# Nine whole expert tiles of the first four batches are run while the last batches are still being routed and ranked

## The reference

```python
x = x + tanh(g_xattn[0]) * xattn(layernorm(x), ctx_2048, mask)       # softmax(x ctx^T / sqrt(512)) ctx
x = x + tanh(g_ffn[0]) * ffn(layernorm(x))

def ffn(x):                                     # T = 2048 tokens
    probs = softmax(xt @ w_router.T)            # 8 experts
    top_v, top_i = top_k(probs, 2)
    top_v = top_v / sum(top_v)
    comb = zeros(T, 8).at[token, top_i].add(top_v)
    g = einsum('th,eih->tei', xt, w_gate)
    u = einsum('th,eih->tei', xt, w_up)
    return einsum('tei,ehi,te->th', silu(g) * u, w_down, comb)
```

## Time and profile before

| | |
|---|---|
| median of 3 runs | 293.11 us (292.9 to 294.67) |
| the profiled execution's own time | 292.34 us |
| its span | 290.5 us |
| mean granted TensorE clock | 0.944 of full |
| TensorE busy | 254.5 us (88%) |
| VectorE busy | 172.3 us (59%) |
| ScalarE busy | 147.4 us (51%) |
| GpSimd busy | 163.8 us (56%) |
| moved by DMA | 52.08 MB, 179 GB/s on average |

### The profile page before, as it was taken

One profiled execution on the slowest core, in us unless ns is written; L12 is line 12 of the kernel. 1 busy time (PEld: TensorE's weight loads), 2 busy tenths in 40 slices (PEclk: granted clock), 3 DMA queues, 4 the chain that ended last, 5 costly groups with the idle time before them and its releaser, 6 DMA issues.

```text
span 290.5 us, 5453 instructions
## 1 busy us (share of the span) xinstructions
PE 254.5 (88%) x1501; PEld 216.1 (74%) x1501; DVE 172.3 (59%) x650; ACT 147.4 (51%) x310; POOL 163.8 (56%) x151
## 2 busy tenths in 40 slices
PE   0999998999999975366999999999999999999940
PEld 1777875687777645356899999899999999999920
DVE  4477779999987899970444444444444554444420
ACT  3469865787765645300455554454444455444430
POOL 1256557556564448316066686874857747748460
PEclk9999999999999978557999999999999999999985
DMA  6996999789988229006157576885985858958582
GB/s 219 381 386 192 325 353 282 295 265 336 301 302 296 82 104 287 4 1 184 38 81 145 103 136 123 143 143 94 171 178 93 168 114 143 154 98 163 109 142 36
DMA packets 25950, 52.08 MB, mean 179 GB/s; under 512 B 5248, under 2 KB 5376, under 8 KB 25920
## 3 DMA queue, kind: packets, MB, share of 16 engines
q0 software_dynamic: 8304, 19.83, 37.0%
q1 hardware_dynamic: 13008, 23.50, 24.7%
q10 hardware_dynamic: 4608, 8.39, 7.6%
HBM read 33.81 MB, written 17.89 MB: 178 GB/s over the span
## 4 chain that ended last, share of the span: by engine, by line
PE 63%; DVE 23%; issue 5%; ACT 3%; DMA 2%; POOL 1%; ACTq 0%; POOLq 0%; DVEq 0%
PE S L1073 9%; PE S L1074 9%; PE S L1077 9%; PE A L1063 5%; PE PO L946 4%; DVE st L609 4%; PE S L935 4%; DVE X L655 3%; DVE TB L721 3%; DVE TA L714 2%; PE PL L1096 2%; DVE dd L675 2%; PE PO L1098 1%; PE PO L1096 1%; PE PL L1100 1%
## 5 line engine op out<-in xcount | busy, mean ns | idle before, releaser
L435 POOL DMA_INDIRECT out<-YT,IXI x36 | 56.8, 1577 | 42.1 <-issue 20.1
L1073 PE MATMUL S<-WGh,XTh 128*128 x144 | 52.3, 363 | 0.9 <-issue 0.8
L1074 PE MATMUL S<-WGl,XTh 128*128 x144 | 49.3, 342 | 0.0
L409 POOL DMA_INDIRECT XG<-x2s,IXG x39 | 38.5, 986 | 18.0 <-issue 9.4
L875 DVE TENSOR_TENSOR H<-SG,S 128x192 f32<-128x192 f32 x36 | 12.7, 354 | 48.5 <-ACT SG L548 40.9
L379 POOL TENSOR_TENSOR WGl<-WGl,WGh 128x512 fp32r<-128x512 f32 x24 | 30.6, 1280 | 14.9 <-ACT WGh L504 14.8
L548 ACT ACTIVATE SG<-S 128x192 f32<-128x192 f32 x36 | 11.9, 330 | 50.3 <-PE S L1077 47.6
L370 POOL TENSOR_TENSOR rs<-mv,CS 128x1 f32<-128x1 f32 x32 | 17.6, 551 | 31.2 <-DVE mv L615 31.2
L946 PE MATMUL PO<-CX,PT 128*128 128x512 f32 x64 | 32.8, 637 | 2.0 <-ACT PT L477 2.0
L868 DVE TENSOR_TENSOR XTl<-A,XTh 128x512 fp32r<-128x512 f32 x37 | 25.6, 691 | 13.0 <-ACT XTh L541 7.9
L1077 PE MATMUL S<-WGh,XTl 128*128 x144 | 31.3, 340 | 0.0
(11 more groups left out here) (153 smaller groups left out, 535.8 us busy)
## 6 DMA issues: line engine op xcount, KB each, us to landing
WGl<-in_wgu SPq DMA_DIRECT2D x24, 256.0 KB, 6.2
X<-in_x SPq DMA_DIRECT2D x16, 256.0 KB, 5.3
CT<-in_ctxt SPq DMA_DIRECT2D x8, 512.0 KB, 6.7
CX<-in_ctxn SPq DMA_DIRECT2D x8, 512.0 KB, 5.4
out<-X ACTq DMA_DIRECT2D x16, 256.0 KB, 5.7
x2s<-Y ACTq DMA_DIRECT2D x16, 256.0 KB, 5.2
WD1l<-in_wd SPq DMA_DIRECT2D x8, 256.0 KB, 5.6
WS<-in_wd SPq DMA_DIRECT2D x8, 256.0 KB, 4.6
```

Of the source, the lines that this page charges most:

```text
L409: pool.indirect_dma_start(out=XG[:, j % NX, :], out_offset=None, in_=x2s, in_offset=bass.IndirectOffsetOnAxis(ap=IXG[:, j:j + 1], axis=0))\
L435: pool.indirect_dma_start(out=out, out_offset=bass.IndirectOffsetOnAxis(ap=IXI[:, j:j + 1], axis=0), in_=YT[:, j % NB, :], in_offset=None, ...
L1073: pe.matmul(o, XTh[:, j % 2, c, :], WGh[:, bass.ds(e, 1), c, :], start=(c == 0), stop=False)
L1074: pe.matmul(o, XTh[:, j % 2, c, :], WGl[:, bass.ds(e, 1), c, :], start=False, stop=False)
```

## The change

The list is made in two parts. After batch 3, `whole()` counts only full tiles of 128 slots in the first four batches; at least 9 exist (`NE = 4 * EB - 7`), and the first 9 go into `IXE` and `ERE`, while the other batches are still in the pipeline. The attention loops stop after step 16; what was left of the tail (attention of tiles 14 and 15, the routing of the last tiles, the ranking of batches 4 to 7, the second list `IXG`, `IXI`, `ERL` with up to 30 tiles) is put by hand into the first tiles of the expert stage, on VectorE by the table `SIDES` (steps before `xlo`, before `hlo` and after it, for each tile). All 40 weight units are now handled in the attention stage, three a step. The scatter index of the early tiles is the same as their gather index.

PSUM is used more tightly, since both kinds of work run together: `tx` has one bank, `th` writes into the bank of `gu`, `down` has one bank. Result buffers are seven, two of them in `WS`. The first gathers wait for the stores that read the `X` slot under their buffer. In GpSimd's queue the gather of tile j+8 follows the add of tile j (before: j+6). An add now always waits for the add two tiles back; it waits for its neighbour only where the expert changes and the first tokens and last tokens of the two tiles allow a common token. Of `exp` for the mixing weights, batches 6 and 7 go to GpSimd as powers of e (`odds`). The two groups of warm-up matmuls ahead of the expert stage (15 and 32) are gone.

```diff
-NB = 5
+NB = 7
-SPLIT = [0, 1, 1] + [2] * 15 + [1] * 4
-NUA = NU - 4
-HOLD = [3, 5, 7, 9]
+SPLIT = [0, 1, 2] + [3] * 12 + [1]
+EB = 4
+NE = 4 * EB - 7
+NL = 32
+SIDES = [(2, 2, 5), (2, 2, 3), (1, 1, 2), (1, 1, 2), (2, 2, 2), (2, 2, 3), (1, 3, 4), (2, 1, 4)] + [(0, 0, 0)] * 31
...
+            def stored(*tiles):
+                pool.wait_ge(s_y2, max(tiles) + 1)
+                for k in tiles:
+                    pool.wait_ge(s_so[k % NXT], 16 * (k // NXT + 1))
+            def fence(j):
+                bits, i = (early, j - 1) if j < NE else (turns[(j - NE - 1) // 15], (j - NE - 1) % 15)
+                with pool.If((bits & (1 << i)) != 0):
+                    landed(j - 1)
...
+                if s == NTK:
+                    pool.wait_ge(s_ixe, 1)
+                    pool.wait_ge(s_sy[0], 16 * EB)
+                    pool.wait_ge(s_sy[1], 16 * EB)
+                    pool.wait_ge(s_scb[0], 16 * EB)
+                    stored(9, 10)
+                    gather(0)
...
                     pool.wait_ge(s_y, j + 1)
-                    if j:
-                        fence(j)
+                    if j >= 2:
+                        landed(j - 2)
+                    if j == NE:
+                        landed(j - 1)
+                    elif j:
+                        fence(j)
...
+                    if j + NX + 2 == NE:
+                        pool.wait_ge(s_ixg, 1)
+                        pool.wait_ge(s_sy[0], 16 * 8)
+                        pool.wait_ge(s_sy[1], 16 * 8)
+                        pool.wait_ge(s_scb[1], 16 * (B - EB))
+                    if j + NX + 2 < NT:
+                        gather(j + NX + 2)
...
+            tp(14)
+            first_list()
+            score(15)
+            pv(14)
+            rt(12)
+            t2(13)
+            tp(15)
...
+            tx(0)
+            pv(15)
+            rt(13)
+            own, live = experts(0, ERE, 0), None
+            pe.wait_ge(s_wl, NU)
             for j in range(NT):
                 with lives(pe, live, j):
                     gu(j, own[j])
+                    if j == 0:
+                        t2(14)
+                    if j == 1:
+                        t2(15)
+                        rt(14)
                     if j + 1 < NT:
                         tx(j + 1)
+                    if j == 0:
+                        cum(5)
+                    if j == 2:
+                        tab(5)
+                        cum(6)
+                    if j == 4:
+                        cum(7)
+                        count()
+                    if j == 5:
+                        tab(6)
+                    if j == 6:
+                        last_list()
+                        tab(7)
...
                     if j >= 1:
                         down(j - 1, own[j - 1])
+                    if j == 1:
+                        rt(15)
+                    if j == 6:
+                        last_rows()
                     th(j)
+                    if j == 0:
+                        tab(4)
```

More of the change, by code:

```diff
@@ L266, in units @@
         def units(s):
-            return range(*[min(NUA, sum(SPLIT[:max(0, n)])) for n in (s, s + 1)])
+            return range(*[min(NU, sum(SPLIT[:max(0, n)])) for n in (s, s + 1)])
         def rows(to, k):
@@ L411, in gather, with landed @@
                     .then_inc(s_g[j % NX], 16)
[L413 to L424 removed]
+            def landed(j):
+                pool.wait_ge(s_add[j % NB], 16 * (j // NB + 1))
@@ L425, in _ @@
+            stored(11)
+            gather(1)
+            rstd(mv2, 14, rs2, s_st2, s_rs2)
+            stored(12)
+            gather(2)
+            rstd(mv2, 15, rs2, s_st2, s_rs2)
+            odds(6)
+            stored(13)
+            gather(3)
+            pool.wait_ge(s_tne, 1)
+            early = pool.value_load(TNE[0:1, 0:1], min_val=0, max_val=(1 << 13) - 1)
+            stored(14, 15)
+            for j in range(4, NX):
                 gather(j)
-            pool.wait_ge(s_tn, 1)
@@ L887, in coef @@
                     dve.wait_ge(s_y, j - 3)
-                link(dve.tensor_tensor(cj8[:, j % 2, :], XG[:, j % NX, D:DW], EJ[:, j, :], ALU.mult))
+                link(dve.tensor_tensor(cj8[:, j % 2, :], XG[:, xg(j), D:DW], EJ[:, j, :], ALU.mult))
                 dve.reduce_sum(cj[:, j % 4:j % 4 + 1], cj8[:, j % 2, :], AX.X).then_inc(s_cj, 1)
-            xlo(0)
+            for s in range(NTK + 1):
+                main = []
+                if s == NTK:
+                    main.append(first_rows())
+                if 0 <= s - 3 < NTK:
+                    main.append(x2(s - 3))
+                if s == NTK:
+                    main.append(first_experts())
+                if s + 2 < NTK:
+                    main.append(st1(s + 2))
+                if 0 <= s - 3 < NTK:
+                    main.append(nbias(mv2, rs2, nb2, s - 3, s_rs2, s_nb2))
+                if s == 2 * EB + 7:
+                    main.append(table())
+                if 0 <= s - 1 < NTK:
+                    main.append(rowmax(s - 1))
+                if s + 2 < NTK:
+                    main.append(nbias(mv1, rs1, nb1, s + 2, s_rs1, s_nb1))
+                if 0 <= s - 1 < NTK:
+                    main.append(norm(s - 1))
+                if s == 2 * EB + 4:
+                    side.append(slots(EB - 2))
+                if s >= 6 and s % 2 == 0:
+                    side.append(top2((s - 6) // 2))
+                if s == 2 * EB + 5:
+                    side.append(braid(slots(EB - 1), whole()))
+                if s >= 8 and s % 2 == 0 and s not in (2 * EB + 4, 2 * EB + 6):
+                    side.append(slots((s - 8) // 2))
+                if s >= 6 and s % 2 == 0:
+                    side.append(ranks((s - 6) // 2))
+                if s >= 7 and s % 2 == 1:
+                    side.append(coefs((s - 7) // 2))
+                weave(queue(*main), s >= 2 * EB + 4)
@@ new lines, in steps, with first_xlo @@
+            def steps(n):
+                for _ in range(n):
+                    while side and next(side[0], side) is side:
+                        side.pop(0)
+            def first_xlo():
+                xlo(0)
+                yield
+            side += [coefs(5), top2(6), taken()]
+            weave(queue(x2(14), first_xlo(), nbias(mv2, rs2, nb2, 14, s_rs2, s_nb2), x2(15)), 2)
+            side += [slots(5), ranks(6), coefs(6),
+                     braid(slots(6), queue(top2(7), braid(ranks(7), coefs(7)))),
+                     braid(slots(7), left()), last_tiles()]
@@ L1025, in _ @@
-                if 0 <= s - 3 < NTK:
-                    t2(s - 3)
-                if s >= 7 and s % 2 == 1 and (s - 7) // 2 < B and s != NTK + 3:
-                    cum((s - 7) // 2)
-                if s == 2 * B + 5:
-                    pe.wait_ge(s_ms, B)
-                    pe.wait_ge(s_lc, B - 1)
-                    for t in range(2 * RB, 2 * B):
-                        pe.matmul(PL[:, 0:8], onesb, MS[:, t // 2, t % 2, :], start=(t == 2 * RB), stop=False)
-                    pe.matmul(PL[:, 0:8], onesb, Rn[:, RB, :], start=False, stop=True).then_inc(s_cnt, 1)
```

645 lines of the change are left out of this document (387 added, 258 removed).

## The result

| | before | after |
|---|---|---|
| median | 293.0 us (4 runs) | 300.82 us (298.31 to 302.35, 4 runs) |
| ratio | | 1.0254, 95% interval 1.0214 to 1.0294 |
| profiled execution, its span | 292.34, 290.5 us | 300.13, 298.3 us |

280.3 us was forecast. The span can be cut at five places that can be read off TensorE's queue. `tp(14)` and the transposes of gathered tiles (`tx`) are marks that both kernels have; "forecast" is the prediction's sum, moved from the first expert matmul to the transpose ahead of it (1.4 us before it).

What follows compares the result with a forecast made beforehand. TensorE was taken to bound both stages, with a VectorE ranking chain making the gap between them. Pieces 96.2 + 5 + 11.5 + 46.4 + 109.5 + 9.9 gave a 278.5 us span, 280.3 us forecast; range 271 to 289.5.

Steps and rivals of the forecast that it cites:

- Piece 1: Attention stage up to tp(14): 96.2 us plus 5 for the third weight unit, bounds 0 and 14.
- (a): GpSimd's queue has room, but 13 more subtractions hold up VectorE by 0.33 us each, 4.3 us.
- (c): Attention-stage DMA: 2.10 MB a step becomes a second bound of equal height; late loads cost a little now and then.
- Each subtraction blocks in full: Rival, attention stage: each of 13 subtractions stops VectorE for its length, 14 instead of 5 us, 289.3; chance 0.16.
- The rival in series: Attention stage: third unit's rounding and subtraction both unhidden in the step's chain, 23.5 instead of 5 us, 298.8; chance 0.06.
- piece 4: Other 27 expert tiles: 109.5 us; the adds' new rule moves nothing, their 3.29 us wait being hidden GpSimd idle time.
- Piece 2 and 3: From tp(14) to the first expert matmul, 11.5 us; then nine early tiles with the moved side work, 46.4 us.
- Piece 5: Tail after the last matmul (last yev, last add and its landing): 9.9 us, unchanged.
- Faster: Whole kernel faster by over 1%: forecast, nothing gives way, late start and over half of full blocking; chance 0.87.
- The signs that I named beforehand: Wrong if attention steps exceed 6.7 us, TensorE awaits last list or gather 9, clock falls to 0.50, yev awaits adds.

Runs made afterwards that it cites:

- e7: Changed kernel with the subtraction of every third weight unit (12 units) cut to 8 of 512 columns, loads and roundings kept: 286.89 us, ratio 0.9767.
- e1: Kernel before with only three weight units a step added (36 by step 13), no early tiles: 298.58 us, ratio 1.0196.
- e2: Changed kernel with the third subtraction of a step moved behind the step's second power in GpSimd's queue: 296.55 us, ratio 1.0141.
- e11: e9 and e8 together, on the changed kernel, both leaving out what they do: 278.94 us, ratio 0.9512.
- e9: e7 with the top-two search of batch 3 put ahead of batch 2's slots in VectorE's ranking work in step 12: 284.13 us, ratio 0.9719.
- e8: Changed kernel with its first nine adds sent to spare rows, without their neighbour waits (results left out): 297.22 us.
- e3: Changed kernel with GpSimd's wait for the second list moved from behind add 1 to behind add 5, two gathers an add after it: 305.99 us, ratio 1.047.
- e10: Changed kernel, whole computation, with the third subtraction behind the second power and batch 3's top-two search first in step 12: 294.10 us, ratio 1.0016.

## Why the prediction was wrong

*What bounds the kernel.* Right: the gap was a chain on VectorE, and it went: `tp(14)` to `tx(0)` fell from 37.1 to 8.4 us.

*Piece 1, up to `tp(14)`: the step that failed.* "I take 5: the 4.3 of (a), and a little for (c)"; it was 21.8, over the upper bound of 14. Three things were wrong in it.
- The price. I took the mean holding up of VectorE for each subtraction (9.0 / 27 = 0.33) and added it up. e7 measured 1.0 us for each of twelve, e1 1.6 for each of nine in the old kernel, with their loads and roundings; why e1's is higher is not shown. By the estimate above an added subtraction held VectorE up for 0.9 us (11.5 / 13; in e1 (18.5 - 9.4) / 9 = 1.0), three times the mean. That mean came from two subtractions a step, one ahead of each power. The third made two in a row ahead of the second power, so that two instructions were held in turn and the power of the next tile came behind them, as the step above shows. e2 prices this place at 4.3 of A's 13.9 us. That the other subtractions of a step had been mostly hidden, and this one could not be, fits these sums, but no run tests it.
- The bound. "Each subtraction blocks in full" (14 us) counted the instruction that is held, not what stands in order behind it (the bias, ScalarE's `Y`, the power of the other tile), nor TensorE's clock behind an idle stretch. The rival in series, 298.8 us at a chance of 0.06, came within 2 us of the result, but its total met it by luck: the moved ranking and piece 4 made part of the loss, and it had nothing on them. Its place was right, GpSimd's subtraction on the step's path. How much that cost by itself lies between e7's 12 to 14 us and the 21 of e1's rate (13 x 1.6), beside its 23.5; none of it is the rounding, which e7 kept while its steps 6 to 11 were 0.2 us longer than before.
- The moved ranking. Up to `tp(14)` I gave it no price at all, since I took the diff's double rate for filling. One search moved was worth 5.5 us of `tp(14)` in the profiled executions (105.60 to 100.06; e11, with the same attention stage as e9, has 101.89, which makes it 3.7) and 2.8 in the medians. With A and this gone `tp(14)` is still 3.9 to 5.7 us later than before, of which step 13 makes 2.8. That this is near my 5 is luck: I had put 4.3 of them on the very subtractions that these runs leave out.

DMA, my (c), took no part that can be seen, as e7 shows. The estimated 5.9 us that the prediction drew from 358 GB/s was no floor for a step: over 14 us of e7 this core moved 376 GB/s, at which the step's 2.10 MB take 5.6 us.

*Piece 2 and 3.* Right: 57.9 us forecast for both, 55.1 measured up to the first matmul of tile 9. The side work fits under the nine tiles; the tightened PSUM shows in no wait (TensorE's longest from `tx(0)` to `tx(9)` is 1.43 us, for tile 0's product `H`). The second list came in time for TensorE: gather 9 started 34.6 us after the first expert matmul, where I had the list at about 33. GpSimd stood still 11.64 us for it, which I had put down as harmless.

*Piece 4.* "The adds' new rule moves nothing on this path" was wrong by 5.9 us. I took the wait of 3.29 us for rare and hidden, which it is behind add 9, in the long runs of one expert. Among the first nine it is not rare: seven adds stood behind the list, and four of them and add 9 waited, so that GpSimd, which came out of its stop with little lead, lost the rest. I had priced gather 9 and not gathers 12 to 17. e8 and e3 show it from both sides.

*Piece 5.* Right, 9.9 and 10.1.

*The chances.* Faster had 0.87, all of it on piece 1, for which I had one indirect row. The signs that I named beforehand did show: steps longer than 6.7 us, and waits for gathers (of tiles 12 to 17, not of tile 9). The clock's lower level showed too, behind idle stretches of the attention stage, which was not the place that I had named. Longer `MS` and `comb` did not show.

## What to carry to other kernels

When work is added to an engine that "has room" inside a software pipeline, look for what it will stand in front of, on its own queue and on any engine that it excludes; price it at its full length, until a gap behind which it can hide is found in the order of instructions. Then place it behind the last short instruction that others wait for. Two orders, on GpSimd and VectorE, were worth 6.7 us here, and a third some 1 to 2.

Work moved forward takes its own waits along: dependent accumulating adds were hidden in a long run and bound the pipeline in a short one. Count the lead that is left when the wait ends, not only whether the first item is in time.

## What the runs showed of the hardware

- An indirect add of 128 rows of 2 KB that must wait for the one before costs 5.6 to 5.8 us from issue to issue (1.55 us of GpSimd and 4.1 to 4.3 us until it has landed, e3), an independent add and gather 3.2 us (e8).
- After waits of TensorE of 2.68 us (e1), 2.93 (e7) and 3.87 (e10) a following group ran at about half its speed (`pv` 3.66 and 3.38 us instead of 1.88, `score` 3.41 instead of 1.89), at granted clocks of 0.51, 0.57 and 0.54, so a wait can cost more than its length. It doesn't always: behind e9's wait of 2.96 us the clock stayed at 1.00 and the next `t1` took its usual 0.60.
- Beside GpSimd's subtractions not only instructions with two SBUF tensors were stretched, but also `TB` (one tensor and two scalars a partition, in single precision): 565 ns in the mean instead of 381, and 1.30 us in one that started at 75.65, 0.07 us behind a subtraction of 1.28 us, where others took 0.33.
- Two subtractions a step held VectorE up for an estimated 0.35 us each (9.4 / 27, before), the third for 0.9 to 1.0 (after and e1). More holding up did not mean a longer path: e2's VectorE was held up for 22.9 us against 20.9 in the changed kernel, and `tp(14)` came 4.0 us earlier.
